# Edge attention over a graph: unused slots of a gather skipped, and TensorE's transposes of gathered rows moved ahead of the weighted sum

## Chip, cores and metric

One Trainium2 chip, one core of it, one launch. The metric is the device time in microseconds (us) of that core, from its first to its last instruction; lower is better. All arrays are fp32 unless said otherwise.

## What is computed

A graph layer over 6250 nodes with 206250 directed edges sorted by destination, then a mixture of small multilayer perceptrons. The change lies in the attention of the graph layer:

```python
q = (x @ Wq.T + bq).reshape(n, 8, 32); k = ...; v = ...      # x normalized, 256 wide, 8 heads
e = (edge_attr @ We.T).reshape(-1, 8, 32)                    # edge_attr: 206250 x 64
alpha = sum(q[dst] * (k[src] + e), -1) / sqrt(32)
alpha = softmax of alpha over the edges of one dst
out = segment_sum((v[src] + e) * alpha[..., None], dst)      # 6250 x 256
```

Behind it come a gate with a skip projection, two layer norms, a feed-forward part and the gated experts, which the change does not touch.

## The kernel before

It has three stages. Stage 1 normalizes x, computes q, k and v for all nodes and stores them in DRAM: `kv_rows` has one row of 512 numbers (2 KB) a node, k and v. It also finds, for every **oct** (8 nodes that follow each other), the place of its first edge. Stage 2, the long one, is the attention. Stage 3 is dense work a node.

Stage 2 takes one **group** of 16 nodes (two octs, o = 0 and 1) at a time: 49 blocks of 8 groups, j = 0 to 7, 392 groups. Each oct has 320 edge slots from its first edge on, whatever its true number of edges (206250 edges over 784 octs are 263 on the mean), so a group has 640 slots, 5 tiles of 128. A slot that belongs to another node gets the weight exp(-1e30) = 0 by a mask. For one group:

- SP (SyncE) loads the source indices (`srci`), the destination numbers and the transposed edge attributes (`F3`).
- POOL (GpSimd) gathers the k and v rows of the group: five indirect DMAs (L597) of 128 rows into `F[s]`, with four slots s in turn. It waits for `slot_free`: the gather for group j+4 starts when group j's weighted sum is done.
- PE (TensorE) transposes the k part of the gathered rows two groups ahead, in three batches `ft(.., 0)`, `ft(.., 1)`, `ft(.., 2)` of 4, 4 and 2 transposes (L828), into the two PSUM banks `ring0` and `ring1`. ACT (ScalarE) copies each batch to `FT` (L760), which gives the bank back (`ring_emptied`). So `ft(.., 2)` waits until ACT has copied `ft(.., 0)`.
- `scores` (L841, L844): q against `FT`, and the edge part `G3` against `F3`, into `pS`. The heads' rows are laid out so that every matmul has 32 output rows, 4 of them side by side. Then DVE (VectorE) takes the maximum `nmx` (L656), ACT the exponential `Pw` (L766), PE transposes it (`pt`, L850), DVE copies it to `PT` (L662).
- `z_part(s, t)` for t = 0, 1, 2 (L860): the weighted sum of v and edge attributes into `pZ`. The last one signals `slot_free` to POOL.

The order of every engine is written out by hand; nothing reorders it. In the loop PE does, for group j: scores of group j+1; in some groups extra work (`project` at j = 1, `g3` at j = 2 and 5, L818); then this:

```python
                                    for t in range(KB):
                                        z = z_part(s, t)
                                        if t == KB - 1:
                                            z.then_inc(slot_free, 1)
                                        if t == 0:
                                            pe.wait_ge(gathered[s2], it * (16 * T * 2) + 16 * T * ((j + 2) // SLOTS + 1))
                                        pe.wait_ge(ring_emptied, rb + (m + t - 1))
                                        ft(s2, t, RING0 + m + t)
```

then `ea_rows` (L867), `pt`, `zt` (L873, L874), and the next group. ACT's order in a group is: copy of `ft(.., 0)`, exponential, copies of `ft(.., 1)` and `ft(.., 2)`, copy of `pZ`, edge rows. DVE's: mask compare `neq` (L650), `join_indices` (L642), maximum, copy to `PT`.

Of the kernel before, what the change touches and what calls it, by code (L numbers as in the profile page):

```python
# [45 lines left out]
def build(nc, a, out):  # L46
# [40 lines left out]
    BLK = DE  # L87
    ZW = P + DE
    K3 = DE + GN
    BC = -(-(NO + 1) // P)  # L90

# [28 lines left out]
    with top:  # L120
# [15 lines left out]
        with mid:  # L136
# [4 lines left out]
            G3 = [sbt(mid, f"G3{i}", [P, KD, HP // ON, C]) for i in range(2)]  # L141
            WeP = sbt(mid, "WeP", [P, HR, 2 * C])
            sel_ready = sem("sel_ready")

            with ExitStack() as s1:
# [25 lines left out]
                srow = sbt(s1, "srow", [1, BC * P], I32)  # L171
                srowf = sbt(s1, "srowf", [1, BC * P])
# [24 lines left out]
                with nc.Block() as block:  # L197
                    @block.sync
                    def _(sp):
# [8 lines left out]
                        for at, v0, v1 in ((2, 0, 1), (5, 1, 2), (6, 2, 4)):  # L208
                            sp.dma_start(Wkv[:, :, at * BLK:(at + v1 - v0) * BLK], wv[:, :, v0 * BLK:v1 * BLK]).then_inc(wv_landed, 16)
                            sp.dma_start(bkv[:, at * BLK:(at + v1 - v0) * BLK], a["bv"][v0 * BLK:v1 * BLK].partition_broadcast(P)  # L210
                                         ).then_inc(bias_landed, 16)
# [3 lines left out]
                        for o in range(KD):  # L215
                            sp.dma_start(bkv[:, o * 3 * BLK:o * 3 * BLK + P], bk_d[o * P:(o + 1) * P].partition_broadcast(P)
                                         ).then_inc(bias_landed, 16)
# [15 lines left out]
                        sp.dma_start(srow[:, :], bound_d.rearrange("(a n) -> a n", a=1)).then_inc(bounds_landed, 16)  # L233
                        for i in range(N7):
# [18 lines left out]
                    def _(pool):  # L253
# [17 lines left out]
                        for b8 in range(0, P, ON):  # L271
                            o = b8 // C % 2
                            chp.step(pool.affine_select(out=seln[:, o * ON:(o + 1) * ON], in_=seln[:, o * ON:(o + 1) * ON],
                                                        compare_op=ALU.not_equal, fill=1.0, base=-b8, pattern=[[-1, ON]],
                                                        channel_multiplier=1))
                        chp.step(pool.memset(selh[:, :], 0.0))
                        for c in range(KD):
                            for o in range(2):
                                for n in range(ON):
                                    chp.step(pool.affine_select(  # L280
                                        out=selh[:, c * HR:(c + 1) * HR], in_=selh[:, c * HR:(c + 1) * HR],
                                        compare_op=ALU.not_equal, fill=1.0, base=-(c * HP + o * C + n),
# [10 lines left out]
                        for i in range(2):  # L293
                            chp.step(pool.memset(G3[i][:, :, :, :], 0.0))
                            for o in range(2):
                                for h in range(HR):
                                    g3 = G3[i][:, :, :, :].rearrange("p c (g o) r -> p (c g) o r", o=2)[:, :, o, h * ON:(h + 1) * ON]
                                    chp.step(pool.affine_select(out=g3, in_=g3, compare_op=ALU.not_equal, fill=-BIG, base=-(DE + o * ON),
                                                                pattern=[[0, KD * HP // GN], [-1, ON]], channel_multiplier=1))
# [9 lines left out]
                    def _(dve):  # L309
# [56 lines left out]
                        dve.wait_ge(bias_landed, 16 * (3 + KD))  # L366
                        for i in range(N7):
# [3 lines left out]
                            if i == 0:  # L371
                                dve.wait_ge(bounds_landed, 16)
# [4 lines left out]
                                ch.step(dve.tensor_scalar(offs[:, 0:NO], srowf[:, 0:NO], float(E), None, ALU.min))  # L377

                    @block.scalar
                    def _(act):  # L380
                        ch = Chain(act, "act1")
                        act.wait_ge(wv_landed, 48)
                        for f in range(KD):
                            act.wait_ge(tp_filled, f + 1)
                            act.activation(Wkv[:, f, 0:6 * BLK].rearrange("p (o c) -> p o c", c=3 * BLK)[:, :, 0:P],
                                           tp[f % 2][:, 0:KD * P].rearrange("p (o c) -> p o c", c=P), ACT.Copy).then_inc(tp_emptied, 1)
# [72 lines left out]
            with ExitStack() as s2:  # L459
                F = [sbt(s2, f"F{i}", [P, T, FP]) for i in range(SLOTS)]  # L460
                F3 = [sbt(s2, f"F3{i}", [P, CH]) for i in range(SLOTS)]
                srci = [sbt(s2, f"srci{i}", [P, 2 * KB], I32) for i in range(GB)]
                FT = [sbt(s2, f"FT{i}", [P, KD, CH]) for i in range(2)]
# [52 lines left out]
                blank = sem("blank")  # L516
# [982 lines left out]
```

## Time and profile before

| | us |
|---|---|
| three runs of the kernel before | 4981.60, 4986.42, 4991.56 (median 4986.42) |
| the profiled execution: its own time | 4956.95 |
| its span, first to last instruction | 4954.7 |
| stage 2's loop in it | 238.6 to about 3697 |
| granted TensorE clock, mean over the span | 0.845 of 2.4 GHz |

A row of the timeline has the start, the duration, the engine, the line in the kernel, the operation and its tiles; in brackets how long the engine had been idle before it and what ended that. A matmul's duration there is modelled from its issue, so when its result was seen is read from the engine that waited for it. "remote" stands where the profile cannot name the instruction that ended a wait.

### The profile page before, as it was taken

The numbers are of one execution on the slowest core, as the hardware profiler recorded it, in microseconds if no ns is written. First come the engines' busy times: TensorE is split into PE (matmuls) and PEld (weight loads), VectorE is DVE, ScalarE is ACT, GpSimd is POOL, SyncE is SP. The second block draws the span as 40 slices with busy tenths as digits, with TensorE's granted clock in tenths as the row PEclk, the third lists the DMA queues.
The fourth block names the chain that finished last, engine by engine and source line by source line (L and its number), as shares of the span: only waits on it lengthen the run. The fifth ranks groups of instructions, "written<-read, shape, count | busy, mean of one in ns | idle before, by whom it ended". The sixth has DMA issues, their size and how long they took to land. (4 is left out here: it accounts for less than half of the span.)

```text
span 4954.7 us, 86461 instructions
## 1 busy us (share of the span) xinstructions
PE 3986.7 (80%) x28082; PEld 2157.7 (44%) x28082; DVE 1796.9 (36%) x4770; ACT 1483.9 (30%) x3644; POOL 1938.6 (39%) x2075
## 2 busy tenths in 40 slices
PE   6787888888888888888888888888867778778778
PEld 3344444444444444444444444444434445445445
DVE  5233333333333333333333333333335454544553
ACT  2133232222232233232332323223223323323322
POOL 2255555555555555555555555555530000000000
PEclk9788888888898888888889898888888778868877
DMA  5566666666666666666666666666660000000000
GB/s 191 161 180 179 172 172 172 175 170 169 181 179 172 168 176 170 173 174 173 173 171 182 178 183 179 172 171 177 170 165 18 15 15 15 15 15 15 15 15 7
DMA packets 638315, 665.65 MB, mean 134 GB/s; under 512 B 408275, under 2 KB 501908, under 8 KB 638244
## 3 DMA queue, kind: packets, MB, share of 16 engines
q0 software_dynamic: 159520, 523.41, 34.7%
q1 hardware_dynamic: 478740, 141.70, 13.9%
q14 instruction: 43, 0.35, 0.0%
q8 instruction: 12, 0.20, 0.0%
HBM read 632.59 MB, written 33.05 MB: 134 GB/s over the span
## 5 line engine op out<-in xcount | busy, mean ns | idle before, releaser
L597 POOL DMA_INDIRECT F<-kv_rows,srci x1970 | 1894.3, 962 | 1622.8 <-PE pZ L860 970.7
L760 ACT ACTIVATE FT<-ring 128x512 f32<-128x512 f32 (+1 forms) x1182 | 581.8, 526 | 1890.4 <-PE ring L828 1005.9
L828 PE MATMUL ring<-ident,F 128*128 128x128 f32 x3940 | 752.2, 309 | 407.8 <-ACT FT L760 392.5
L860 PE MATMUL pZ<-F,PT 128*32 128x192 f32 x9408 | 793.2, 362 | 117.6 <-issue 114.2
L828 PEld LDWEIGHTS ring<-ident,F 128*128 128x128 f32 x3940 | 447.1, 151 | 859.0 <-ACT FT L760 565.7
L656 DVE TENSOR_REDUCE nmx<-pS 128x1 f32<-128x384 f32 x393 | 219.3, 558 | 1263.3 <-remote 1098.9
L662 DVE COPY PT<-pPT 128x384 f32<-128x384 f32 x393 | 219.2, 558 | 956.6 <-issue 522.9
L860 PEld LDWEIGHTS pZ<-F,PT 128*32 128x32 f32 x9408 | 263.2, 116 | 483.0 <-issue 442.2
L1106 POOL DMA_DIRECT2D out_dram<-accb x6 | 5.8, 960 | 1077.8 <-DVEq L1271 1077.8
L841 PE MATMUL pS<-FT,qh 128*32 128x320 f32 x3144 | 382.6, 567 | 17.9 <-issue 14.2
L844 PE MATMUL pS<-F,G 80*32 80x320 f32 x3144 | 386.5, 571 | 0.0
L650 DVE TENSOR_SCALAR F<-F,nid 16x640 f32<-16x640 int32 x394 | 224.2, 569 | 41.5 <-issue 26.1
L850 PE MATMUL pPT<-ident,Pw 128*128 128x128 f32 x1179 | 236.0, 313 | 0.9 <-ACT Pw L766 0.9
L1382 PE MATMUL hid<-rT,W1T 128*128 128x512 f32 (+1 forms) x448 | 204.9, 617 | 35.6 <-ACT h L1314 27.9
L766 ACT ACTIVATE Pw<-pS,nMn 128x384 f32<-128x384 f32 x393 | 226.4, 576 | 7.6 <-DVE nMn L657 3.3
L778 ACT ACTIVATE G<-pM 64x512 f32<-64x512 f32 x99 | 58.6, 592 | 563.3 <-remote 380.6
L867 PE MATMUL pM<-ident,F 64*128 64x64 f32 x1965 | 213.5, 240 | 0.6
L844 PEld LDWEIGHTS pS<-F,G 80*32 80x32 f32 x3144 | 127.8, 140 | 171.9 <-issue 109.9
L1390 PE MATMUL nat<-W2T,h 128*128 128x256 f32 x784 | 176.3, 386 | 27.1 <-ACT h L1314 27.1
L867 PEld LDWEIGHTS pM<-ident,F 64*128 64x128 f32 x1965 | 158.2, 144 | 75.5 <-issue 75.5
L873 PE MATMUL pZv<-ident,Zs 128*128 128x128 f32 x392 | 137.8, 351 | 63.4 <-issue 55.0
L1287 ACT ACTIVATE rT<-tr 128x256 f32<-128x256 f32 x147 | 54.4, 384 | 436.8 <-PE tr L1373 434.9
(200 smaller groups left out, 4427.7 us busy)
## 6 DMA issues: line engine op xcount, KB each, us to landing
F<-in_edge_attrT SPq DMA_DIRECT2D x788, 80.0 KB
F<-kv_rows,srci POOLq DMA_INDIRECT x1970
F<-in_dst SPq DMA_DIRECT2D x788, 20.0 KB
srci<-src_front SPq DMA_DIRECT2D x796, 1.5 KB
kv_rows<-kvs SPq DMA_DIRECT2D x7, 1792.0 KB, 6.4
qb<-q_cols SPq DMA_DIRECT2D x100, 64.0 KB
U<-in_x SPq DMA_DIRECT2D x7, 896.0 KB, 10.9
xn_rows<-xs SPq DMA_DIRECT2D x7, 896.0 KB, 6.3
```

The source lines that it names most:

```text
L597: pool.indirect_dma_start(out=F[s][:, t, 0:KV], out_offset=None, in_=kv_d, in_offset=bass.IndirectOffsetOnAxis(ap=srci[j % GB][:, col:col ...
L650: dve.tensor_scalar(F3[j][DE:K3, :], F3[j][DE:K3, :].bitcast(I32), nid[DE:K3, c], None, ALU.not_equal).then_inc(neq_done, 1)
L656: ch.step(dve.tensor_reduce(nmx[:, j:j + 1], pS[:, 0:SW], AX.X, ALU.max, negate=True))
L662: dve.tensor_copy(PT[:, :, :], pPT[:, 0:SW].rearrange("p (t r) -> p t r", r=P)).then_inc(pt_emptied, 1)
L760: act.activation(FT[j % 2][:, :, t0 * P:t1 * P], ring[n % 2][:, 0:KD * w].rearrange("p (k e) -> p k e", e=w), ACT.Copy).then_inc(ring_empt ...
L766: act.activation(Pw[:, :], pS[:, 0:SW], ACT.Exp, bias=nMn[:, j:j + 1], accum_out=lsum[:, j:j + 1]).then_inc(p_done, 1)
L828: m = pe.transpose(ring[n % 2][:, k * w + (t - t0) * P:k * w + (t - t0 + 1) * P], F[j][:, t, k * 3 * BLK:k * 3 * BLK + P], ident[:, :])
L841: m = pe.matmul(pS[rows, cols], qh[half][:, c, g + o, :], FT[j % 2][:, c, o * OW:(o + 1) * OW], start=True, stop=False)
L844: m = pe.matmul(pS[rows, cols], G3[half][0:K3, c, g + o, :], F3[s][0:K3, o * OW:(o + 1) * OW], start=False, stop=True)
L850: m = pe.transpose(pPT[:, t * P:(t + 1) * P], Pw[:, t * P:(t + 1) * P], ident[:, :])
L860: m = pe.matmul(pZ[rows, 0:ZW].rearrange("p (x d) -> p x d", d=BLK), PT[:, t, rows], f, start=(t == 0), stop=(t == KB - 1))
L867: m = pe.transpose(pM[:, t * DE:(t + 1) * DE], F3[s][0:DE, t * P:(t + 1) * P], ident[0:DE, 0:DE])
```

## The change

Three things are done together.

1. **Rows behind an oct's last edge are not gathered.** DVE computes, for every slot, position minus the oct's length, scaled so that a slot behind the end gets an index above the table; the gather has a bounds check that drops such rows. What stays in `F` is what was there before, so `F` is cleared once ahead of the first gather. 250880 slots for 206250 edges: 17.8% of the gathered rows are left out. The number of indirect DMAs stays 5 a group.
2. **The rows of pS and pZ are ordered by oct first, then by half of the heads.** The edge parts of scores and weighted sum become matmuls with 64 output rows (2 side by side); the q and v parts keep 32 (4 side by side).
3. **All three `ft` batches stand ahead of the three z parts** (lines 968 to 977 of the changed kernel), so `slot_free` is signalled behind them all.

In the core of the diff, `...` marks what is left out (stage 1's loads in fewer pieces, the selection tables, the same reordering where outputs are copied out).

```diff
+    SKIP = float(1 << 17)
...
+                        sp.dma_start(brow[:, :], bound_d[0:NO + 1].partition_broadcast(P)).then_inc(bounds_landed, 16)
...
+                            chp.step(pool.iota(posb[:, o * KB:(o + 1) * KB], pattern=[[P, KB]], base=-o * HP, channel_multiplier=1,
+                                               allow_small_or_imprecise_dtypes=True))
+                        chp.step(pool.tensor_scalar(posb[:, :], posb[:, :], 0.5, SKIP, ALU.add, ALU.mult))
...
+                                ch.step(dve.tensor_copy(browf[:, :], brow[:, :]))
+                                ch.step(dve.tensor_sub(lenb[:, 0:NO], browf[:, 1:NO + 1], browf[:, 0:NO]))
+                                ch.step(dve.tensor_scalar(lenb[:, 0:NO], lenb[:, 0:NO], SKIP, None, ALU.mult))
...
                                 pool.indirect_dma_start(
                                     out=F[s][:, t, 0:KV], out_offset=None, in_=kv_d,
-                                    in_offset=bass.IndirectOffsetOnAxis(ap=srci[j % GB][:, col:col + 1], axis=0),
+                                    in_offset=bass.IndirectOffsetOnAxis(ap=srcg[j % GB][:, col:col + 1], axis=0),
+                                    bounds_check=NP - 1, oob_is_err=False,
                                 ).then_inc(gathered[s], 16)
 
+                        pool.wait_ge(blank, 10)
                         for j in range(2):
                             pool.wait_ge(idx_ready, j + 1)
...
+                        for s in range(SLOTS):
+                            dve.memset(F[s][:, :, 0:KV], 0.0).then_inc(blank, 1)
...
-                            dve.tensor_copy(srci[j][HP:P, KB - 1:KB], srci[j][HP:P, KB:KB + 1]).then_inc(idx_ready, 1)
-
+                            for o in range(2):
+                                w = slice(o * KB, (o + 1) * KB)
+                                dve.scalar_tensor_tensor(out=srcg[j][:, w], in0=posb[:, w], scalar=lenb[:, first(o)], in1=srci[j][:, w],
+                                                         op0=ALU.subtract, op1=ALU.max).then_inc(cut, 1)
+                            cuts[0] += 2
+                            dve.wait_ge(cut, cuts[1] + cuts[0])
+                            dve.tensor_copy(srcg[j][HP:P, KB - 1:KB], srcg[j][HP:P, KB:KB + 1]).then_inc(idx_ready, 1)
...
-                            for x in range(2):
-                                for c in range(KD):
-                                    for o in range(2):
-                                        r = c * HP + o * C
-                                        rows, cols = slice(r, r + C), slice(o * HP, o * HP + OW)
-                                        if x == 0:
-                                            m = pe.matmul(pS[rows, cols], qh[half][:, c, g + o, :],
-                                                          FT[j % 2][:, c, o * OW:(o + 1) * OW], start=True, stop=False)
-                                        else:
-                                            m = pe.matmul(pS[rows, cols], G3[half][0:K3, c, g + o, :],
-                                                          F3[s][0:K3, o * OW:(o + 1) * OW], start=False, stop=True)
+                            for c in range(KD):
+                                for o in range(2):
+                                    r = o * HP + c * C
+                                    pe.matmul(pS[r:r + C, o * HP:o * HP + OW], qh[half][:, c, g + o, :],
+                                              FT[j % 2][:, c, o * OW:(o + 1) * OW], start=True, stop=False)
+                            for o in range(2):
+                                m = pe.matmul(pS[o * HP:(o + 1) * HP, o * HP:o * HP + OW],
+                                              G3[half][0:K3, g + o, :, :].rearrange("p c r -> p (c r)"),
+                                              F3[s][0:K3, o * OW:(o + 1) * OW], start=False, stop=True)
                             m.then_inc(s_done, 1)
...
-                                    rows = slice(c * HP + o * C, c * HP + (o + 1) * C)
-                                    blocks = F[s][:, o * TO + t, :].rearrange("p (x d) -> p x d", d=BLK)
-                                    f = blocks[:, 2:9:3, :] if c == 0 else blocks[:, 6:9, :]
-                                    m = pe.matmul(pZ[rows, 0:ZW].rearrange("p (x d) -> p x d", d=BLK), PT[:, t, rows], f,
-                                                  start=(t == 0), stop=(t == KB - 1))
+                                    rows = slice(o * HP + c * C, o * HP + (c + 1) * C)
+                                    pe.matmul(pZ[rows, 0:P], PT[:, t, rows], F[s][:, o * TO + t, D + c * P:D + (c + 1) * P],
+                                              start=(t == 0), stop=False)
+                            for o in range(2):
+                                rows = slice(o * HP, (o + 1) * HP)
+                                m = pe.matmul(pZ[rows, P:ZW], PT[:, t, rows], F[s][:, o * TO + t, KV:FP], start=False, stop=(t == KB - 1))
                             return m
 
                         def ea_rows(s):
...
+                                    pe.wait_ge(gathered[s2], it * (16 * T * 2) + 16 * T * ((j + 2) // SLOTS + 1))
+                                    for q in range(len(PAIRS)):
+                                        pe.wait_ge(ring_emptied, rb + (m + q - 1))
+                                        ft(s2, q, RING0 + m + q)
+
                                     pe.wait_ge(pt_emptied, it * GB + (j + 1))
                                     pe.wait_ge(z_out, it * GB + (j + 1))
                                     for t in range(KB):
                                         z = z_part(s, t)
-                                        if t == KB - 1:
-                                            z.then_inc(slot_free, 1)
-                                        if t == 0:
-                                            pe.wait_ge(gathered[s2], it * (16 * T * 2) + 16 * T * ((j + 2) // SLOTS + 1))
-                                        pe.wait_ge(ring_emptied, rb + (m + t - 1))
-                                        ft(s2, t, RING0 + m + t)
+                                    z.then_inc(slot_free, 1)
```

How the order of PE's instructions moves, one group without extra work (j = 0): scores of group 1, then transposes of `F2` (two groups ahead) and the weighted sum of `F0`. `pS`, `pZ`, `ring0`, `ring1`, `pPT` are PSUM banks. Before:

```order
L841 MATMUL pS<-FT1,qh1 32x320 x4
L844 MATMUL pS<-F31,G31 32x320 x4
L860 MATMUL pZ<-F0,PT 32x192 x4
L948 REGISTER_ALU
L828 MATMUL ring0<-ident,F2 128x128 x4
L860 MATMUL pZ<-F0,PT 32x192 x4
L828 MATMUL ring1<-ident,F2 128x128 x4
L860 MATMUL pZ<-F0,PT 32x192 x4
L948 REGISTER_ALU
L828 MATMUL ring0<-ident,F2 128x128 x2
L867 MATMUL pM<-ident,F30 128x64 x5
```

The same stretch of the changed program:

```order
L867 MATMUL pS<-FT1,qh1 32x320 x4
L870 MATMUL pS<-F31,G31 64x320 x2
L970 REGISTER_ALU
L857 MATMUL ring0<-ident,F2 128x128 x4
L857 MATMUL ring1<-ident,F2 128x128 x4
L970 REGISTER_ALU
L857 MATMUL ring0<-ident,F2 128x128 x2
L885 MATMUL pZ<-F0,PT 32x128 x4
L889 MATMUL pZ<-F0,PT 64x64 x2
```

The last two rows stand three times in the changed program. All of the weighted sum now stands behind the third batch into ring0, which needs ring0 copied out by ACT; before, all of it stood ahead of that batch. The gathered rows of group j+2 are needed before any of it instead of behind its first third.

On DVE, the place between the mask compare and the maximum of the next group. Before:

```order
L650 TENSOR_SCALAR F<-F,nid 16x640
L642 COPY srci<-srci 64x1
L655 REGISTER_ALU
L656 TENSOR_REDUCE nmx<-pS 128x1
L118 REGISTER_ALU
```

The changed program has there:

```order
L674 TENSOR_SCALAR F<-F,nid 16x640
L660 ISA
L660 SCALAR_TENSOR_TENSOR srcg<-posb,lenb,srci 128x3
L660 ISA
L660 SCALAR_TENSOR_TENSOR srcg<-posb,lenb,srci 128x3
L663 REGISTER_ALU
L664 COPY srcg<-srcg 64x1
L679 REGISTER_ALU
L680 TENSOR_REDUCE nmx<-pS 128x1
```

Two small operations and a wait for them have come in ahead of the maximum.

## Rows read from the trace of the kernel before

**Rows 1.** The page: busy time, share of the span and instructions.

```profile
PE 3986.7 (80%) x28082; PEld 2157.7 (44%) x28082; DVE 1796.9 (36%) x4770; ACT 1483.9 (30%) x3644; POOL 1938.6 (39%) x2075
```

**Rows 2.** Windows: length, busy us of PE, PEld, DVE, ACT, POOL, clock, DMA, GB/s.

```profile
238.63:3697.00 3458.37, 2850.51 (x24657) 1456.36 (x24656) 1100.90 (x3089) 1037.46 (x2886) 1875.38 (x1952) 0.86 0.64 174
```

**Rows 3.** The waits: who waited for whom, total us, times, longest.

```profile
DVE nmx L656 <- remote: 1098.9, 332, 5.2
...
PE ring L828 <- ACT FT L760: 392.5, 321, 3.6
```

**Rows 4.** The timeline of two groups, j = 1 and j = 2.

```profile
2505.52 0.66 PE L828 MATMUL ring<-ident,F 128*128 128x128 f32 x4
...
2506.11 0.53 PE L860 MATMUL pZ<-F,PT 128*32 128x192 f32 x8
2506.22 0.60 ACT L760 ACTIVATE FT<-ring 128x512 f32<-128x512 f32 x1 [6.03 <-PE ring L828]
...
2506.57 0.66 PE L828 MATMUL ring<-ident,F 128*128 128x128 f32 x4
...
2507.16 0.53 PE L860 MATMUL pZ<-F,PT 128*32 128x192 f32 x8
...
2508.60 0.95 POOL L597 DMA_INDIRECT F<-kv_rows,srci  x1 [3.82 <-PE pZ L860]
...
2509.13 0.75 PE L841 MATMUL pS<-FT,qh 128*32 128x320 f32 x8
...
2511.82 0.66 PE L828 MATMUL ring<-ident,F 128*128 128x128 f32 x4
2512.18 0.56 DVE L656 TENSOR_REDUCE nmx<-pS 128x1 f32<-128x384 f32 x1 [1.96 <-remote]
...
2512.93 0.59 ACT L778 ACTIVATE G<-pM 64x512 f32<-64x512 f32 x1 [3.90 <-PE pM L818]
...
2513.46 0.53 PE L860 MATMUL pZ<-F,PT 128*32 128x192 f32 x8
...
2515.86 0.60 ACT L760 ACTIVATE FT<-ring 128x512 f32<-128x512 f32 x1 [2.33 <-remote]
...
2516.51 0.44 PE L828 MATMUL ring<-ident,F 128*128 128x128 f32 x2 [2.52 <-ACT FT L760]
...
2516.92 0.95 POOL L597 DMA_INDIRECT F<-kv_rows,srci  x1 [2.18 <-remote]
```

**Rows 5.** The timeline, the four groups behind them.

```profile
2523.30 0.56 DVE L656 TENSOR_REDUCE nmx<-pS 128x1 f32<-128x384 f32 x1 [3.81 <-remote]
...
2524.13 0.60 ACT L760 ACTIVATE FT<-ring 128x512 f32<-128x512 f32 x1 [5.80 <-PE ring L828]
...
2525.20 0.95 POOL L597 DMA_INDIRECT F<-kv_rows,srci  x1 [2.28 <-PE pZ L860]
...
2532.42 0.60 ACT L760 ACTIVATE FT<-ring 128x512 f32<-128x512 f32 x1 [5.83 <-remote]
...
2533.49 0.95 POOL L597 DMA_INDIRECT F<-kv_rows,srci  x1 [2.29 <-PE pZ L860]
...
2540.63 0.59 ACT L778 ACTIVATE G<-pM 64x512 f32<-64x512 f32 x1 [5.74 <-PE pM L818]
...
2543.85 0.95 POOL L597 DMA_INDIRECT F<-kv_rows,srci  x1 [4.36 <-PE pZ L860]
...
2551.01 0.60 ACT L760 ACTIVATE FT<-ring 128x512 f32<-128x512 f32 x1 [6.73 <-remote]
```

**Rows 6.** Source line L597: ns min/median/max, first, last start; who waited for it.

```profile
L597 POOL DMA_INDIRECT F<-kv_rows,srci x1970: 943/949/1244, 196.2 to 3667.1; - x197
...
  PEld ring L828: 2.6, 1
```

**Rows 7.** The timeline at the start of stage 2.

```profile
192.47 0.48 DVE L627 MEMSET pZv<- 128x512 f32 x1 [0.18 <-issue]
...
196.23 0.97 POOL L597 DMA_INDIRECT F<-kv_rows,srci  x1 [45.37 <-DVE srci L642]
```

## What I expect of the change

> **What bounds the kernel now.** I read the page first, then windows of the second stage, the waits, and last the timeline of six groups, which decided. PE is busy 80% of the span and no other engine over 39% [rows 1]; in the loop of stage 2 PE has 2850.5 of 3458.4 us, at a granted clock of 0.86 (it changes between 1.2 and 2.4 GHz), and DMA a share of 0.64 [rows 2]. That looks like a kernel bound by TensorE with room for transfers. The loop takes (3667.1 - 238.6 - 5.1)/391 = 8.76 us a group; 238.6 is where its window begins, 3667.1 the last of its indirect DMAs, 5.1 us the distance from the first to the last of five (1.25 each and a little) [rows 2, 6].
>
> The waits do not fit a PE bound: DVE waits 1098.9 us for a maximum's input, from "remote", 332 times, and PE waits 392.5 us in 321 cases until ACT has copied a ring [rows 3]. The timeline shows why. The reader is to compare where PE's matmuls end with where the engine that waits for them starts. When POOL is idle they meet: `ft(.., 0)` is over at 2505.52 + 0.66 = 2506.18, ACT starts at 2506.22 [rows 4]. With POOL's gathers under way (from 2508.60 on, five of them) they do not: `ft(.., 0)` is over at 2512.48 and ACT starts at 2515.86, 3.4 us late; the last z part is over at 2513.99 and POOL, which only waits for it, starts at 2516.92 [rows 4]. So results of PE are seen late behind a batch of gathers. The lateness has a fixed end: from the first gather of a batch to ACT's copy of `ft(.., 0)` are 2515.86 - 2508.60 = 7.26, then 7.21 (from 2516.92), 7.22 and 7.16 us [rows 4, 5], whatever the clock or PE's own place. From that copy to the next batch's first gather are 1.06, 1.07 and 1.07 us. This closes a ring of 7.2 + 1.07 = 8.28 us, and the batches do stand 8.32, 8.28 and 8.29 us apart, 10.36 where `g3` of j = 5 lies between [rows 4, 5]. **The loop is bound by this ring: gathers hold back what PE has done, and the last z part, which is done long before, frees the slot as soon as the hold ends.** Which part of a gather holds PE's signals the profile does not say.
>
> Not everything is held to the end. The scores' maximum starts 3.58 us behind the first gather in one group, 6.38 in the next; a `g3` batch, issued right behind scores, is seen after 4.33 us once and after 7.14 us another time (2512.93 - 2508.60; 2540.63 - 2533.49) [rows 4, 5]. `ft(.., 0)`, behind scores and a z part, never came before 7.16 in these groups.
>
> **The change part by part.** *Order.* Now z stands behind `ft(.., 2)`, which waits for ACT's copy of `ft(.., 0)`. If `ft(.., 0)` is seen only at 7.2, what used to be finished is still to do: 0.65 us until `ft(.., 2)` starts (2515.86 to 2516.51), 0.44 for it, three z parts, and 0.91 to POOL's start (2507.69 to 2508.60) [rows 4]. A z part takes 0.46 us from its start to the next batch (2506.11 to 2506.57) [rows 4]; now each has 12 matmul passes of fewer columns instead of 8 and a change from 32 to 64 output columns inside. No row shows that; its bounds are 0.46 and 0.46 + 0.46, if the narrow matmuls cost as much as the whole now. I take 0.55, nearer to the lower, as the columns streamed stay 192 for each side-by-side set: 1.65 us in all. The ring would be 7.2 + 0.65 + 0.44 + 1.65 + 0.91 = 10.85 us. If `ft(.., 0)` is seen at about 4.3, like the first `g3`, z is over at 4.3 + 0.65 + 0.44 + 1.65 = 7.04, is held to 7.2, and the ring is 8.28 as now.
>
> Which of both? When z comes last, the gathers start 0.91 us behind it and the next scores some 1.4 us behind it (`ea_rows`, `pt`, `zt` lie between), so a batch starts 0.5 us ahead of scores, as it does in the group at 2509.13, whose `g3` came at 4.33 [rows 4]. `ft(.., 0)` takes the place of `g3` there. At the lower clock scores take twice as long and it falls further into the hold. I take it as early in 7 of 10 of the groups with nothing between (five of eight). At j = 1 `project` and at j = 5 `g3` stand ahead: late, 10.85. At j = 2 `g3` is seen at 4.3 and `ft(.., 0)` some 0.7 behind: 5.0 + 0.65 + 0.44 + 1.65 + 1.07 = 8.8. Mean: (5 x (0.7 x 8.28 + 0.3 x 10.85) + 2 x 10.85 + 8.8)/8 = 9.47 us, 0.71 above 8.76, and 392 x 0.71 = +278 us.
>
> *TensorE's forms.* Changes of matmul shape between neighbours go from 6 to 9 a group (32 to 64 in scores, five inside z). The Trainium skill (TensorEngine Tiling (Array Packing), Key Properties) says that changing the tiling mode drains the engine. By it each z part and scores pay a drain that none paid inside before, and with z at its upper bound of 0.92 the late ring would be 11.96 us, 435 us more if every group were late. I keep 0.55, as the sum above does.
>
> *Skipped rows.* 17.8% fewer rows move. DMA share is 0.64 [rows 2], and PE waited once for a gather in the whole run, 2.6 us [rows 6], so the bytes alone buy nothing. Order needs them one z part earlier and frees the slot later; with a ring of 8 us or more that leaves them their present time. The five gathers take 0.95 us each on POOL and stay five [rows 6]; a bounds check can make one longer, which no row shows. Bounds: 0 and +0.29, the longest of 1970 now against the median (1.24 - 0.95) [rows 6]; I take 0, since neither the instructions nor their 128 indices each change in number. The Trainium skill (Perfetto Trace Analysis, DMA Instruction — SWDGE (GPSIMD)) says that POOL's row ends with the last descriptor made, not with the data moved. So these 0.95 us would not show the bytes saved, by that rule; the hold might, which is a rival below.
>
> *DVE.* Two operations of 3 numbers a partition and a wait come in ahead of the maximum. Each is under the 0.48 us that 512 numbers take [rows 7], so all under 1 us. DVE is idle 1.96 and 3.81 us at that place [rows 4, 5], which hides them. Were scores seen at once, they would put up to 1 us on the exponential's side; the ring covers that too.
>
> *Start.* Clearing F: 4 x 2560 numbers a partition at 0.48 us for 512 [rows 7] is 9.6 us, on DVE, ahead of the first gather at 196.23, for which POOL already waits 45.37 us for DVE [rows 7]: +10 us. The 16 more selections on POOL in stage 1 lie in those 45 us.
>
> **Sum.** The profiled execution has 4956.95 us, 0.6% under the median of 4986.42. I add to the median: 4986 + 278 + 10 = 5274, say 5270 us.
>
> **The rivals.**
> - *Late everywhere* (0.13): if `ft(.., 0)` is never seen ahead of the hold's end, as it was never in the six groups: 392 x (10.85 - 8.76) + 10 = +829, 5815 us.
> - *Early everywhere* (0.17), the other side: the ring is 8.28 in all groups, also those with `project`, since nothing of z waits behind it: 392 x (8.28 - 8.76) + 10 = -178, 4808 us. It decides where fewer than 2 in 10 groups are late (0.48/2.57). For it speaks the first `g3`; against it the second.
> - *The hold shrinks with the rows* (0.10): 5.1 of its 7.2 us pass from the first to the last gather; if that span is a matter of rows, a sixth less is -0.9 us: on top of some late groups 392 x -0.9 = -350, 4640 us.
> - *The check makes gathers longer* (0.09) with `ft(.., 0)` early: +0.2 us each is +1.0 a group: 4808 + 392 = 5200 us.
> - *Gains and losses cancel* (0.06), within 10 us of 4986.
>
> **How the numbers follow.** My forecast has 0.45: 5270, its own range 5090 (all five plain groups early) to 5460 (4 of 10 early). The whole range leaves out the late-everywhere case and most of the shrinking hold, 2 in 10: 4700 to 5620. Within 0.2% (10 us) is about what a measurement can't tell from no change. Faster: 0.17 + 0.10 = 0.27; same 0.06; slower 0.45 + 0.13 + 0.09 = 0.67.
>
> **What the changed profile would show.** Right: first gathers of batches 8.3 us apart in some groups and 10 to 11 in others; PE waits for ACT's ring copy with all z parts behind it; POOL's idle time before a gather grows. Early case: ACT copies `ft(.., 0)` some 4 us behind the first gather. Wrong, if batches stand under 8 us apart, or the copy comes 6.3 instead of 7.2 us behind the first gather, or L610 has a mean well off 0.96. The likeliest error is in the share of early groups: each tenth of the plain groups is 63 us.

## The result and the profile after

The changed kernel takes 5306.14 us (median of 4 runs, 5302.25 to 5314.89), the kernel before 4984.01 beside it: a ratio of 1.0658, interval 1.0619 to 1.0696. It is slower, by 322 us; 5270 was forecast. The profiled execution has 5314.89 us, against 4956.95.

Where the 358 us lie follows from the gathers' row of the source line, as in [rows 6] (ns min/median/max of one, first and last start), and the waits that go with it (total us, times, longest):

```profile
L610 POOL DMA_INDIRECT F<-kv_rows,srcg x1970: 992/998/1313, 207.4 to 4030.8; - x197
```

```profile
DVE PT L686 <- PE pPT L877: 2059.4, 393, 8.8
POOL F L610 <- PE pZ L889: 1372.6, 390, 13.5
...
ACT FT L788 <- PE ring L857: 964.0, 495, 7.8
...
ACT FT L788 <- remote: 586.0, 199, 7.3
```

In the kernel before, POOL's wait was:

```profile
POOL F L597 <- PE pZ L860: 970.7, 332, 17.3
```

The first gather starts at 207.4 instead of 196.2: 11.2 us. From the first to the last are 3823.4 us instead of 3470.9: 352.5 more, 0.90 for each of 392 groups. Behind the last gather 5.2 are given back. All of it is stage 2's loop, and POOL's wait for z grows from 970.7 to 1372.6 us: the slot comes free late. One gather takes 998 instead of 949 ns.

Windows of the loop and of three groups, j = 6, 1 and 2 (length, busy us of PE, PEld, DVE, ACT, POOL, then clock, DMA share, GB/s), to lay beside [rows 2]:

```profile
249.00:4040.00 3791.00, 3126.17 (x27702) 1745.11 (x27700) 1285.17 (x3852) 1152.89 (x2880) 1946.85 (x1949) 0.80 0.52 133
2563.07:2571.63 8.56, 6.30 (x67) 3.62 (x66) 2.47 (x7) 2.67 (x7) 4.99 (x5) 0.94 0.65 157
2591.59:2604.17 12.58, 9.01 (x83) 5.70 (x82) 3.32 (x9) 2.44 (x7) 4.98 (x5) 0.75 0.41 109
2604.17:2613.84 9.67, 8.94 (x77) 4.92 (x75) 2.38 (x7) 3.63 (x9) 4.99 (x5) 0.80 0.55 146
```

The loop moves 133 instead of 174 GB/s and is slower all the same. The groups differ by 4 us. The timeline of POOL for one turn of eight groups, only the first gather of each batch; the distances are the groups j = 3, 4, 5, 6, 7, 0, 1, 2:

```profile
2536.27 1.00 POOL L610 DMA_INDIRECT F<-kv_rows,srcg  x1 [4.17 <-PE pZ L889]
...
2544.72 1.00 POOL L610 DMA_INDIRECT F<-kv_rows,srcg  x1 [2.24 <-PE pZ L889]
...
2553.39 0.99 POOL L610 DMA_INDIRECT F<-kv_rows,srcg  x1 [2.47 <-PE pZ L889]
...
2563.07 1.00 POOL L610 DMA_INDIRECT F<-kv_rows,srcg  x1 [3.47 <-PE pZ L889]
...
2571.63 0.99 POOL L610 DMA_INDIRECT F<-kv_rows,srcg  x1 [2.35 <-PE pZ L889]
...
2582.71 0.99 POOL L610 DMA_INDIRECT F<-kv_rows,srcg  x1 [4.80 <-PE pZ L889]
...
2591.59 0.99 POOL L610 DMA_INDIRECT F<-kv_rows,srcg  x1 [2.67 <-PE pZ L889]
...
2604.17 1.00 POOL L610 DMA_INDIRECT F<-kv_rows,srcg  x1 [6.38 <-PE pZ L889]
...
2613.84 1.00 POOL L610 DMA_INDIRECT F<-kv_rows,srcg  x1 [3.46 <-PE pZ L889]
```

They are 8.45, 8.67, 9.68, 8.56, 11.08, 8.88, 12.58 and 9.67 us: 9.70 on the mean. One turn is a small sample. Over the 49 turns of both traces the mean distance from the first gather of batch j to that of the next, and PE's busy time in between, are (us):

| j | 0 | 1 | 2 | 3 | 4 | 5 | 6 | 7 |
|---|---|---|---|---|---|---|---|---|
| before | 8.78 | 10.93 | 8.38 | 8.30 | 8.28 | 9.10 | 8.39 | 8.48 |
| after | 9.16 | 12.54 | 10.67 | 8.55 | 8.70 | 9.16 | 8.82 | 10.24 |
| PE busy before | 6.34 | 10.50 | 6.48 | 6.99 | 6.03 | 8.38 | 6.15 | 7.39 |
| PE busy after | 8.31 | 9.11 | 9.27 | 6.89 | 7.46 | 7.87 | 6.71 | 8.41 |

Of the 7.20 us that a turn is longer, 5.66 lie at j = 1, 2 and 7. At j = 1 PE was busy for nearly the whole group before; now it stands idle for 3.4 us of it.

Now an early group, j = 6, whose first gather starts at 2563.07:

```profile
2564.56 1.09 PE L857 MATMUL ring<-ident,F 128*128 128x128 f32 x8
...
2565.96 0.60 ACT L788 ACTIVATE FT<-ring 128x512 f32<-128x512 f32 x1 [2.92 <-PE ring L857]
...
2566.61 0.44 PE L857 MATMUL ring<-ident,F 128*128 128x128 f32 x2 [0.96 <-issue]
...
2566.98 0.43 PE L885 MATMUL pZ<-F,PT 128*32 128x128 f32 x8
...
2567.60 0.42 PE L885 MATMUL pZ<-F,PT 128*32 128x128 f32 x8
...
2570.32 0.35 PE L889 MATMUL pZ<-F,PT 128*64 128x64 f32 x4 [1.06 <-issue]
```

ACT copies `ft(.., 0)` 2.89 us behind the first gather. The z parts follow at once, the first two 0.62 us each, but the last one's end does not come: PE stands still, waiting for nothing that the profile names, and goes on with its last four matmuls at 2570.32, which is 7.25 behind the first gather. The batch behind it starts at 8.56. And the late group, j = 1, from 2591.59 on:

```profile
2594.89 1.07 PE L857 MATMUL ring<-ident,F 128*128 128x128 f32 x8
...
2598.88 0.60 ACT L788 ACTIVATE FT<-ring 128x512 f32<-128x512 f32 x1 [7.32 <-remote]
...
2599.53 0.69 PE L857 MATMUL ring<-ident,F 128*128 128x128 f32 x2 [3.57 <-ACT FT L788]
...
2600.15 0.65 PE L885 MATMUL pZ<-F,PT 128*32 128x128 f32 x8
...
2601.14 0.66 PE L885 MATMUL pZ<-F,PT 128*32 128x128 f32 x8
...
2603.14 0.79 PE L895 MATMUL pM<-ident,F 64*128 64x64 f32 x5
```

The copy comes at 7.29; then everything that used to be done already is to be done: 0.65 to `ft(.., 2)`, 0.62 for it, 2.99 for three z parts at the lower clock (0.75 in this window), 1.03 to POOL: 12.58 us.

### The profile page after: what moved, and what is told of

Same layout as the page of the kernel before. It is cut to its first block and busy times, and to the rows that moved or that the text cites. A ratio compares the mean times of both kernels' runs of the same rounds, so it can differ in the third digit from the quotient of the medians.

```text
span 5313.2 us, 96854 instructions
## 1 busy us (share of the span) xinstructions
PE 4264.5 (80%) x31214; PEld 2450.5 (46%) x31214; DVE 2002.0 (38%) x5572; ACT 1600.2 (30%) x3644; POOL 2017.4 (38%) x2094
## 3 DMA queue, kind: packets, MB, share of 16 engines
q0 software_dynamic: 159520, 429.57, 28.0%
## 5 line engine op out<-in xcount | busy, mean ns | idle before, releaser
L610 POOL DMA_INDIRECT F<-kv_rows,srcg x1970 | 1968.9, 999 | 1912.7 <-PE pZ L889 1372.6
L857 PE MATMUL ring<-ident,F 128*128 128x128 f32 x3940 | 681.9, 311 | 542.9 <-issue 307.6
L885 PE MATMUL pZ<-F,PT 128*32 128x128 f32 x9408 | 648.3, 326 | 57.1 <-issue 56.7
L889 PE MATMUL pZ<-F,PT 128*64 128x64 f32 x4704 | 469.8, 276 | 70.8 <-issue 70.1
L889 PEld LDWEIGHTS pZ<-F,PT 128*64 128x64 f32 x4704 | 283.8, 157 | 394.1 <-issue 391.7
L870 PE MATMUL pS<-F,G 80*64 80x320 f32 x1572 | 388.7, 582 | 0.0
L885 PEld LDWEIGHTS pZ<-F,PT 128*32 128x32 f32 x9408 | 220.6, 117 | 228.5 <-issue 163.7
L877 PE MATMUL pPT<-ident,Pw 128*128 128x128 f32 x1179 | 278.7, 359 | 2.1 <-ACT Pw L794 2.1
L836 ACT ACTIVATE Zs<-pZ 128x192 f32<-128x192 f32 x392 | 129.6, 331 | 495.5 <-PE pZ L889 495.5
L870 PEld LDWEIGHTS pS<-F,G 80*64 80x64 f32 x1572 | 94.7, 166 | 299.3 <-issue 299.3
```

The lines of the kernel that those rows point to most:

```text
L610: pool.indirect_dma_start(out=F[s][:, t, 0:KV], out_offset=None, in_=kv_d, in_offset=bass.IndirectOffsetOnAxis(ap=srcg[j % GB][:, col:col ...
L857: m = pe.transpose(ring[n % 2][:, k * w + (t - t0) * P:k * w + (t - t0 + 1) * P], F[j][:, t, k * P:(k + 1) * P], ident[:, :])
L870: m = pe.matmul(pS[o * HP:(o + 1) * HP, o * HP:o * HP + OW], G3[half][0:K3, g + o, :, :].rearrange("p c r -> p (c r)"), F3[s][0:K3, o * OW ...
L877: m = pe.transpose(pPT[:, t * P:(t + 1) * P], Pw[:, t * P:(t + 1) * P], ident[:, :])
L885: pe.matmul(pZ[rows, 0:P], PT[:, t, rows], F[s][:, o * TO + t, D + c * P:D + (c + 1) * P], start=(t == 0), stop=False)
L889: m = pe.matmul(pZ[rows, P:ZW], PT[:, t, rows], F[s][:, o * TO + t, KV:FP], start=False, stop=(t == KB - 1))
```

## The experiments

They ran on three chips, four kernels on each, and the kernel before had a median of 4085.96 us on the first, 4992.23 on the second and 4088.19 on the third. The late results of PE do not come with the program: the same one has them on some chips and not on others. Times are compared on one chip only. Each chip was used in one stretch of time, so nothing here tells a property of the chip from one of that stretch; "chip" stands for both below. I call the second chip, like the one of the result, a **holding** chip.

### First chip: each part alone (before: 4085.96 us)

Order alone:

```diff
-                                    for t in range(KB):
-                                        z = z_part(s, t)
...
-                                        ft(s2, t, RING0 + m + t)
+                                    for q in range(len(PAIRS)):
+                                        pe.wait_ge(ring_emptied, rb + (m + q - 1))
+                                        ft(s2, q, RING0 + m + q)
...
+                                    for t in range(KB):
+                                        z = z_part(s, t)
+                                    z.then_inc(slot_free, 1)
```

> Alone on the kernel before: the three ft batches and their waits stand ahead of the three z parts; old layout of pS and pZ, all rows gathered, no bounds check. If the order is what costs (slot_free comes behind the ring's wait and three z parts, so the late groups take 10 to 11 us instead of 8.3), this kernel keeps most of the loss: 5150 to 5300 us. If the loss came from the new forms of z and scores or from the bounds check instead, it stays within 50 us of 4986.

Measured: 4157.88 us, ratio 1.0165 (1.0092 to 1.0238). Neither figure of the expectation could come, since this chip does not hold PE's results. In its timeline `ft(.., 0)` and `ft(.., 1)` go out at 1514.74 (8 matmuls in 1.09, so the first four end at about 1515.4), with gathers under way since 1513.09, and ACT starts at once:

```profile
1513.09 0.95 POOL L597 DMA_INDIRECT F<-kv_rows,srci  x1 [2.27 <-PE pZ L860]
...
1514.74 1.09 PE L828 MATMUL ring<-ident,F 128*128 128x128 f32 x8
...
1515.44 0.60 ACT L760 ACTIVATE FT<-ring 128x512 f32<-128x512 f32 x1 [1.97 <-PE ring L828]
...
1516.45 1.18 PE L860 MATMUL pZ<-F,PT 128*32 128x192 f32 x24
...
1517.57 0.52 PE L867 MATMUL pM<-ident,F 64*128 64x64 f32 x5
```

Batches stand 6.8 us apart here (first gather 195.8, last 2874.4, less 5.0 within a batch, over 393). `ft` needs the gathered rows, z does not, and z now stands behind that wait, so this may be another cost of the order. Its waits:

```profile
PE ring L828 <- DMA F<-kv_rows,srci: 323.6, 260, 3.9
...
POOL F L597 <- PE pZ L860: 224.3, 158, 5.5
```

No trace of the kernel before was taken on a chip of this kind, so by how much the order changed these waits is not shown. The nearest old-order trace, with skipped rows alone (next run), has 278.5 us for the first and 98.8 us for the second: PE's wait for rows is there in the old order too, and what differs is that POOL waits longer for z.

Skipped rows alone:

```diff
-                                    in_offset=bass.IndirectOffsetOnAxis(ap=srci[j % GB][:, col:col + 1], axis=0),
+                                    in_offset=bass.IndirectOffsetOnAxis(ap=srcg[j % GB][:, col:col + 1], axis=0),
+                                    bounds_check=NP - 1, oob_is_err=False,
```

> Alone on the kernel before: rows behind an oct's last edge are not gathered (index made by DVE, bounds check, F cleared once); old layout and old order. If skipped rows buy nothing and the check is free: 4986 + 10 for clearing F = 4996 us. If the check's longer gathers (999 against 949 ns on the mean, five a group) lengthen the time from the first gather to the release of PE's results: 392 x 5 x 0.05 = +98, 5094 us. If fewer rows shorten that hold: 392 x -0.9 = 4640 us.

Measured: 4128.71 us, ratio 1.0122 (1.0044 to 1.0199), +43 us for 17.9% fewer bytes. POOL is the pace on this chip: five gathers and the 0.30 between them are 5 x (1.003 + 0.30) = 6.51 us with the check and 5 x (0.953 + 0.30) = 6.26 without (the second mean from the run with the order alone); the later start adds about 11. If POOL set the pace in every group, that were 392 x 0.25 + 11 = 109 us; 43 are left, so part of it falls into gaps that are there anyway, or the fewer bytes give some back. The run does not separate these two.

Layout alone:

```diff
-                                    m = pe.matmul(pZ[rows, 0:ZW].rearrange("p (x d) -> p x d", d=BLK), PT[:, t, rows], f,
-                                                  start=(t == 0), stop=(t == KB - 1))
...
+                                    pe.matmul(pZ[rows, 0:P], PT[:, t, rows], F[s][:, o * TO + t, D + c * P:D + (c + 1) * P],
+                                              start=(t == 0), stop=False)
+                            for o in range(2):
+                                rows = slice(o * HP, (o + 1) * HP)
+                                m = pe.matmul(pZ[rows, P:ZW], PT[:, t, rows], F[s][:, o * TO + t, KV:FP], start=False, stop=(t == KB - 1))
```

> Alone on the kernel before: rows of pS and pZ ordered by oct first, edge parts of scores and z as matmuls with 64 output rows; old order, all rows gathered. If the gather ring sets the pace, z's longer parts (0.95 against 0.67 us on the mean) lie in the time that the ring leaves: within 20 us of 4986. If PE's own work sets it: 392 x 3 x 0.28 = +330, 5310 us, and the order would be innocent.

Measured: 4188.2 us, ratio 1.0269 (1.0189 to 1.0349), +102 us: the dearest part here, and between the two cases of the expectation, which were priced for a holding chip.

Skip and layout together, so the changed kernel with the old order:

> The changed kernel with the old order of ft and z (z0, ft0, z1, ft1, z2, ft2) put back, nothing else. By the ring theory 4996 to 5100 us, as in the run with the skipped rows alone. If the layout's costs add up with the order's, it is in the middle, 5150 us. If order does nothing, 5306 us as the changed kernel.

Measured: 4148.26 us, ratio 1.014 (1.0068 to 1.0212): with the layout in, the skipped rows cost nothing here. They give some 40 us back: all five runs (4140 to 4169) lie below the four of the layout alone (4173 to 4214). So what skipping is worth depends on what stands beside it; by what path was not looked into.

### Second chip: what holds PE's results (before: 4992.23 us)

> The kernel before, unchanged, for its trace beside the next runs. The four runs so far stood beside a kernel before of 4086 us, with batches of gathers 6.8 us apart, and PE's results were seen at once; the trace of [rows 4, 5] has 8.3 us and results 3 to 4 us late. If the lateness belongs to the chip and not to the program, this kernel takes either about 4086 us with ACT's copy of ft(.., 0) some 3.5 us behind a batch's first gather, or about 4984 with 7.2, and nothing between. If it comes and goes within a chip, single runs differ.

Measured: 4993.36 us in its one run; POOL waits 989.8 us for z in 328 cases. On no chip did a run of the kernel before lie between the two levels, or leave the level of its chip (all lie within 4051 to 4108 or within 4957 to 5021).

> The changed kernel, unchanged. Where before takes about 4086 us: POOL's five gathers fill the whole group there (5 x (0.953 + 0.30) = 6.26 us, 5 x (1.00 + 0.30) = 6.51 with the check), so the kernel is bound by POOL and by what stands between z and the next gather. Each part alone costs 43 (skip), 72 (order) and 102 us (layout); if they add up: 4300 us; if they share one cover (POOL's 6.51 us): about 4190. Where before takes about 4984: 5306 again.

Measured: 5273.49 us, ratio 1.0545 (1.049 to 1.0599). The direction and most of the size again; the interval does not meet that of the result, and no run says why.

Three gathers a group instead of five:

```diff
-                            for t in range(T):
-                                col = t if t < KB else t + 1
+                            for t in range(KB):
+                                col = t
```

> The changed kernel with three gathers a group instead of five: the last two tiles of every group are not gathered (they stay zero), everything else runs as before. Where before takes 4984 us: if PE's results are held until a fixed time behind the last gather, the hold ends 2 x 1.30 = 2.6 us sooner, at 4.7 us behind the first gather, and the kernel takes 5306 - 392 x 1 to 2.6 = 4290 to 4900 us; if the hold does not come from the gathers, 5250 us or more. Where before takes 4086: POOL needs 3.9 us a group and PE's own work is the bound, 392 groups of about 6.6 us, 4050 to 4150 us; if it stays within 30 us of the changed kernel, POOL was not the bound there.

Measured: 4617.76 us, 656 less than the changed kernel, ratio to before 0.9239 (0.9192 to 0.9285). Its timeline, two batches, first and last gather and ACT's copy, in the second with PE's `ft`:

```profile
2603.16 1.00 POOL L610 DMA_INDIRECT F<-kv_rows,srcg  x1 [4.93 <-PE pZ L889]
...
2605.76 1.00 POOL L610 DMA_INDIRECT F<-kv_rows,srcg  x1 [0.30 <-issue]
...
2607.51 0.60 ACT L788 ACTIVATE FT<-ring 128x512 f32<-128x512 f32 x1 [4.02 <-PE ring L857]
...
2611.42 1.00 POOL L610 DMA_INDIRECT F<-kv_rows,srcg  x1 [4.66 <-PE pZ L889]
...
2614.03 1.00 POOL L610 DMA_INDIRECT F<-kv_rows,srcg  x1 [0.30 <-issue]
...
2614.72 1.07 PE L857 MATMUL ring<-ident,F 128*128 128x128 f32 x8
...
2615.90 0.60 ACT L788 ACTIVATE FT<-ring 128x512 f32<-128x512 f32 x1 [4.50 <-PE ring L857]
```

The second batch belongs to j = 1, the group that in the changed kernel has its copy at 7.29: now 4.48. PE issues `ft(.., 0)` 3.30 us behind the first gather in both (2594.89 - 2591.59; 2614.72 - 2611.42), so the place is the same and only the gathers differ. The copy is 2.8 us earlier for 2 x 1.30 us of gathers less. From the start of the last gather to the copy are 1.75 and 1.87 us here and 7.25 - 5.21 = 2.04 in the changed kernel (2568.28 is the last gather of j = 6). So the hold goes with the gathers: it ends about 2 us behind the start of the last. Over the 49 turns j = 1 has its copy at 4.4 to 4.5 in 27; with five gathers it has it at 7.2 or 7.3 in 48. In 17 turns of this run it comes at 8.0; in the one looked at (from 2416.61 on) that is no hold: PE runs at the lower clock, issues `ft(.., 0)` only 6.9 us behind the first gather, and ACT starts as its results are due.

The 4-byte index loads as 12-byte pieces:

```diff
-                            sp.dma_start(s[:, 0:KB], src_t[bass.ds(oa, KB * P)].rearrange("(t p) -> p t", p=P)).then_inc(done, 16)
+                            sp.dma_start(s[:, 0:KB], src_t[bass.ds(oa, KB * P)].rearrange("(p t) -> p t", p=P)).then_inc(done, 16)
...
```

> The changed kernel with the source indices loaded as three neighbours a partition (12 bytes in one piece) instead of 4 bytes each: 128 pieces a load instead of 384, same bytes. Slots then hold other edges' rows than the mask and the edge part belong to (that part of the result changes), the work stays the same. Where before takes 4984 us: if the hold on PE's results comes from these 4-byte pieces, which run 4 to 5.7 us behind the first gather, it ends earlier and the kernel drops by 392 x 0.5 to 1.5 = 200 to 600 us; if it comes from the gathers, within 30 us of the changed kernel. Where before takes 4086: within 30 us of the changed kernel.

Measured: 5262.07 us, 11 below the changed kernel, ratio 1.0525 (1.0468 to 1.0582). The rival source of the hold, the many small pieces that run in its middle, falls: with a third of them, j = 1 still has its copy at 7.2 or 7.3 in 47 of 49 turns.

### Third chip: the parts joined, and the opposite order (before: 4088.19 us)

These were meant for a holding chip, and this one does not hold. Two kernels ran a second time:

> The kernel before with ft ahead of z, nothing else, a second time, wanted where before takes about 4990 us (its results of PE are seen late there). By the prediction's sum with z parts of 0.67 us as the trace of before has them: 392 x 0.7 to 0.9 = 270 to 350 us more, 5260 to 5340. If the longer z parts of the new layout are the greater part of the loss: under 5150. Where before takes about 4086: 1.0165 again.

Measured: 4163.34 us, ratio 1.0201 (1.0147 to 1.0255).

> The changed kernel with the old order of ft and z put back, a second time, wanted where before takes about 4990 us. If order is nearly all of the loss: 4990 + 10 + 392 x 0.05 to 0.25 = 5020 to 5100 us. If the layout's z parts (0.95 against 0.67 us) or the check's gathers make the loss: 5200 to 5300. Where before takes about 4086: 1.014 again.

Measured: 4156.27 us, ratio 1.0168 (1.0115 to 1.022).

Order and layout without the skipped rows:

> The changed kernel without the skipped rows (no bounds check, no index arithmetic, F not cleared, all rows gathered); new layout and new order. Where before takes about 4990: the changed kernel had 1.0545 there; if skipping rows buys nothing and costs clearing F (10 us) and 0.04 us a gather, this is 10 to 90 us faster than the changed kernel, 1.037 to 1.053; if fewer rows did shorten the time for which PE's results are held, it is slower than the changed kernel, over 1.06. Where before takes about 4086: 1.03 to 1.05.

Measured: 4317.88 us, ratio 1.0607 (1.0527 to 1.0687), +230 us, where the two alone have +75 here and +102 on the first chip. They come to more than their sum, 177. Groups by line and form show that z's parts are longer, and they stand behind more: z of the run with the order alone (its trace on the first chip), then of this one (count | busy us, mean ns | idle before):

```profile
L860 PE MATMUL pZ<-F,PT 128*32 128x192 f32 x9264 | 508.1, 357 | 0.0
```

```profile
L875 PE MATMUL pZ<-F,PT 128*32 128x128 f32 x9264 | 509.4, 293 | 0.0
L879 PE MATMUL pZ<-F,PT 128*64 128x64 f32 x4632 | 398.8, 252 | 0.0
```

PE is busy with z for 400 us more (509.4 + 398.8 - 508.1), and POOL waits 409.2 us for it instead of 224.3 (253.2 in the run with the order alone on this chip).

All z parts ahead of all `ft`, on the kernel before:

```diff
                                     for t in range(KB):
                                         z = z_part(s, t)
...
-                                        ft(s2, t, RING0 + m + t)
+                                    z.then_inc(slot_free, 1)
...
+                                    for q in range(len(PAIRS)):
+                                        pe.wait_ge(ring_emptied, rb + (m + q - 1))
+                                        ft(s2, q, RING0 + m + q)
```

> The kernel before with the opposite order: all three z parts, with slot_free, ahead of the three ft batches; nothing else. Where before takes about 4086, POOL needs 6.26 of 8.8 us... its own words: POOL's gathers are the pace and the gaps between batches shrink when z is over earlier: 3960 to 4070 us. Where before takes about 4990 there are two ways. If what matters is only how early z is over, the next batch starts as soon as z is seen, 7.3 to 8.0 us apart instead of 8.9: 4380 to 4640 us. If the copy of PT, whose transposes now fall 2 to 3 us behind the first gather, is seen late instead, z waits for it and the batches stand 7.2 + 0.6 + 1.4 + 0.9 = 10.1 us apart: 5460 us.

Measured: 3974.96 us, ratio 0.9728 (0.9681 to 0.9775): faster than before by 113 us. (The words "6.26 of 8.8" in the expectation mix the two kinds of chip; the figure behind them is that of this kind.) Its waits and gathers:

```profile
PE ring L828 <- DMA F<-kv_rows,srci: 87.0, 159, 3.0
...
POOL F L597 <- PE pZ L860: 32.9, 95, 3.3
```

```profile
L597 POOL DMA_INDIRECT F<-kv_rows,srci x1970: 941/946/1263, 195.8 to 2685.2; - x197
```

(2685.2 - 195.8 - 5.0)/393 = 6.32 us a group, where POOL alone needs 5 x (0.957 + 0.30) = 6.28: the loop runs at POOL's floor.

## Why the prediction came out as it did

- **The ring of 8.28 us: right on a holding chip.** The hold ends at 7.25 to 7.29 again, and is tied to the gathers, as the run with three shows. The prediction took it for the limit of the whole loop. At j = 1 the kernel before is not bound by it: PE is busy for 10.50 of 10.93 us there. And it took it for a property of the kernel, where it comes and goes with the chip; on two other chips the bound is POOL with 6.26 us a group and what stands in its gaps.
- **`slot_free` behind the ring's wait: right, one term mis-sized.** The late group is built as forecast, but takes 12.58 instead of 10.85 us (12.54 on the mean of 49). The step that failed is "I take 0.55, nearer to the lower": a z part takes 0.62 us at the full clock and 0.99 at the lower one. That is 2.99 - 1.65 = 1.34 of the 1.73 us missing; `ft(.., 2)` (0.62 for 0.44), POOL's start (1.03 for 0.91) and the copy (7.29 for 7.2) are the rest. The price of 0.46 was read from one place at the full clock, for a loop at 0.86.
- **Which groups are early: near on the sum, wrong in its parts, and so in part luck.** The five plain groups of the turn shown have 8.88, 8.45, 8.67, 8.56 and 11.08 us, 9.13 on the mean; 9.05 was forecast. Four of them are early, with copies at 2.9 to 4.6 us. In the fifth, j = 7, scores ran at the lower clock and the copy came at 5.79. At j = 5 the copy came at 5.77 and not at 7.2: 9.68 instead of 10.85. At j = 2 it came at 5.76 and not at 5.0: 9.67 instead of 8.8. The turn as a whole: 77.57 us for 75.76. Over all turns the errors are plainer and cancel: j = 5 takes 9.16 us, 1.69 less than forecast, j = 1 1.69 more, and j = 2 10.67, 1.87 more, since its copy comes at 5.8 to 7.3 and never at 5.0. The plain groups have 9.09 on the mean for 9.05, but in another way: nearly 9 in 10 have their copy under 5 us and not 7 in 10, and the early groups take more than 8.28. The fifth, j = 7, shows what the sum had no term for, the clock: in the turn shown it has 0.50 and PE is busy for 10.05 of 11.08 us; over all turns it has 0.66, the lowest of the eight, and 8.41 of 10.24 us. The loop lost 0.90 us a group for 0.71 forecast. A part of that gap is the base: 8.76 divides the time from 238.6, which is no batch's start; from the first gather on, (3667.1 - 196.2 - 5.0)/393 = 8.82.
- **In early groups z is held to 7.2: right, with a trait unforeseen.** PE itself stands still until 7.25 and only then runs its last matmuls, so the ring there is 8.56 in the group shown (8.55 on the mean of j = 3) instead of 8.28.
- **TensorE's forms.** The bounds of a z part's price, 0 and +0.46, hold at the full clock: three old parts in a row take 1517.57 - 1516.45 = 1.12 us, 0.37 each, a new one 0.62. That is 0.25 x 3 x 392 = 294 us of PE's time, for the same 192 columns of each side-by-side set. The Trainium skill (TensorEngine Tiling (Array Packing), Key Properties) has it that a change of mode drains the engine; a part now brings one change inside it and one before the next, and these go with the 0.25 us, though no run separates the changes from the 4 additional matmuls. The sum should have gone nearer to that rule.
- **Skipped rows buy nothing: open on a holding chip. The check is free: wrong.** L610's mean is 999 ns where L597 had 962, one of the prediction's own signs of being wrong. It costs 0.05 us a gather, 0.25 a group on POOL; skipping cost 43 us alone on the first chip and gave 40 back beside the new layout, and on a holding chip its price was not measured apart. The rival of a hold that shrinks with the rows is refuted for the bytes: 17.9% fewer, and the hold ends at 7.25. The packets stayed 159520 in both traces, so whether the hold goes with them is not tested by the skipped rows; three gathers a group have 96480.
- **Start: +10 forecast, +11.2 measured.**
- **DVE's added work is hidden: right in the group shown.** At j = 6 the maximum starts at 2564.96, right behind DVE's index work, and the exponential only at 2566.45, behind ACT's copy.
- Late everywhere is refuted by the copies at 2.9 to 4.6 us. The other side, early everywhere, failed on j = 1: `project` delays `ft(.., 0)` into the hold, and z waits behind it.

Open: how much of the loss on a holding chip is the order's and how much the layout's. Both of the runs that would say it met other chips, and there order and layout together give 1.0607, near to the 1.0658 of the whole change, though nothing is held there. The whole change was never run on such a chip. Why PE's granted clock fell from 0.86 to 0.80 in the loop is open too; at the full clock the late group would have 3 x (0.99 - 0.62) = 1.1 us less for z alone. Also open is what part of a gather stops PE, what differs between the chips, and what z ahead of `ft` would do on a holding chip; neither was tried there.

## What to carry to other kernels

What gives a buffer back to the engine that sets the pace belongs ahead of everything that can wait for something else: on chips that do not hold, moving z behind `ft` cost 72 to 75 us and moving it ahead gained 113. Price a moved block at the clock of its loop, from a row for the whole run, and not from one place, and average over many turns before calling one typical. And run the kernel before on more than one chip before explaining its waits: here a bound of 8.3 us a group existed on one kind of chip only.

## What the hardware showed that was not expected

- Two levels: the same program takes 4086 and 4088 us on two chips, 4984 and 4992 where PE is held (one chip or two). At the higher level, while a batch of indirect DMAs runs, PE's results come through only now and then (2.89 and 4.39 us behind the first gather in the group of 2563.07: ACT's copies at 2565.96 and 2567.46), and its issue stops too, until about 2 us behind the start of the last gather. ACT is not held: its copy of 2565.96 lets PE start `ft(.., 2)` 0.65 us later, at 2566.61, in the middle of it, as it does with no gather under way [rows 4].
- A bounds check makes an indirect DMA of 128 rows 5% longer on POOL (998 for 949 ns), also with every sixth row left out. The Trainium skill (Perfetto Trace Analysis, DMA Instruction — SWDGE (GPSIMD)) has this row end with the last descriptor made; the traces agree in so far as fewer bytes never shortened it.
